# Softmax of the keys with tokens on partitions, their maxima spread by a transfer, in a two-layer linear attention kernel

## The chip, the cores and the metric

The kernel runs on one core of one Trainium2 chip. The metric is the device time of one execution in microseconds (us). A core has TensorE (PE, with its weight loads as PEld), VectorE (DVE), ScalarE (ACT), GpSimd (POOL) and SyncE (SP), which here only issues transfers; each runs its own instructions in the order written, and they wait for each other by semaphores.

## The reference

x has 32 batches of 128 tokens and 512 features. Two layers follow each other; each normalises x, makes queries, keys and values, forms for every head a small matrix from keys and values, applies it to the queries, and ends in a conditioned normalisation and an output product.

```python
xn = layernorm(x)
q = xn @ Wq + bq;  k = xn @ Wk + bk;  v = xn @ Wv + bv
k = where(mask, -inf, k)          # second layer: k + (1 - mask) * -1e6
v = where(mask, 0, v)             # second layer: v * mask
q = softmax(q, axis=-1)           # over the 32 (64) features of a head
k = softmax(k, axis=tokens)       # over the 128 tokens of a batch
attn = einsum('bhse,bhsd->bhed', k, v)
y = einsum('bhtd,bhed->bhte', q, attn)
h = layernorm(y) * (1 + scale) + shift      # scale, shift from the condition
x = x + silu(h) @ Wo + bo
```

The first layer has 16 heads of 32 features, the second 8 of 64. All is float32; the large products are made as three products of a high and a low part (WH, WL for weights, XH, XL for x, HH, HL for h).

## The kernel before

There are 64 steps: batches 0 to 31 of the first layer, then the same of the second, and each engine works through them in a software pipeline. In step s TensorE makes `keys(s)`, `values(s)` and `queries(s)`, `output(s-4)` and `mix(s-2)`; `attention` comes for two batches together in every second step, between queries and output (`attention_at`, TOGETHER). Products are made by `split_product` (line 1152).

Keys are made for a pair of batches at once, turned: a step makes half of the 512 features for both batches of its pair, with features on partitions and 256 tokens in a row, as 24 matmuls of 256 columns. So the softmax over tokens runs along a row. `keys` on VectorE (lines 1575 to 1581) adds the mask, takes the maximum and makes the bias; `exp_k` on ScalarE (829) is four exponentials with their sums; `key_sums` (1587) is the reciprocal, `normalise_keys` on GpSimd (674) the product, `turn_keys` (1596) a turn of 32x32 blocks into KT. Two transfers, out (`write_keys`, `write_half_keys`) and back in four parts (`place_keys`), put tokens on partitions, in EK. `load_mask` and `mask_of_keys` (687, 689) bring the mask to all partitions for each pair. `attention` (1232) writes 16 small products for a batch into the diagonal blocks of a PSUM bank that `zero_attention`, `zero_turned` and `zero_film` keep zero elsewhere, and `heads` on ScalarE (902) copies the bank whole to ATT.

`mix` (1248) multiplies EQ, the exponentials of the turned queries, with ATT. `mixed` on VectorE (1650 to 1664) divides and takes the statistics of y, `root_y` on GpSimd makes the factors, `norm_y` (836) applies them. The queries and y are turned by VectorE into QS (`turn_queries`, `turn_y`), written by `write_qy` and read back into QT by `read_qy`, four transfers behind a wait (434) until `exp_q` (847) and `film` have read the batch before, for QT is one buffer. `film` (867) with its tanh (872) and `h_mul` (1670) make h; `h_high` on ScalarE (916) and `h_low` on GpSimd (680) make HH and HL, for which `output` waits. X is turned in the same manner (`norm_x` 953, `turn_x` 1537, `write_x`, `read_x`, `x_turned` 935 and 942, `x_low` 667), for the pair after. In six steps (2, 3, 9, 13, 17, 21) `conditioning` adds matmuls. Around steps 31 to 36 the weights are changed, and the order there is written out by hand, as at the start and the end.

## Time and profile before

| | us |
|---|---|
| median of 3 runs | 861.52 |
| lowest and highest | 857.33, 862.12 |
| the profiled execution | 857.14 |
| its span, first to last instruction | 855.1 |
| DVE, ACT, POOL busy in the span | 679.3, 603.1, 548.9 |

Busy times are read against the span; the profiled execution has 2.0 us outside its span. It is near the lowest run, 4.4 below the median. The granted TensorE clock was 1.00 throughout, which is 2.4 GHz. A matmul's busy time reaches past the start of the next one, so how long a product takes is read from start to start.

### The profile page before, as it was taken

Reading aid. Unit: us, or ns where it says so; the run is one execution under the profiler, and the core shown is the slowest. Engines: PE = TensorE matmul, PEld = TensorE weight load, DVE = VectorE, ACT = ScalarE, POOL = GpSimd, SP = SyncE. Lnnn points to the kernel's source line nnn. Section 1 sums busy time; section 2 is a strip of 40 time slices with the busy share of each in tenths; the row PEclk is TensorE's granted clock in tenths of the full one; section 3 lists DMA queues with packets and bytes.
Section 4 is the critical chain, followed back from the end, with each engine's and each line's share of the span. In section 5 each row is a group of like instructions: output and inputs, shape, how many; then the busy total and the mean of one; then the engine's idle time right before and its main releaser. Section 6 shows DMA issues by size and latency. Waiting matters only on the chain.

```text
span 855.1 us, 20095 instructions
## 1 busy us (share of the span) xinstructions
PE 838.2 (98%) x6659; PEld 719.9 (84%) x6659; DVE 679.3 (79%) x1362; ACT 603.1 (71%) x1442; POOL 548.9 (64%) x741
## 2 busy tenths in 40 slices
PE   7999999999999999999999999999999999999998
PEld 7778888888888888888878888888888888888886
DVE  6987778778788788778887887787788787787766
ACT  5376687686676776686876886776776686676665
POOL 3467766766766666766767667667667666765641
PEclk9999999999999999999999999999999999999999
DMA  8876676766667756555587556656566656566441
GB/s 309 286 225 201 201 218 199 228 216 205 195 210 208 233 197 199 179 165 175 169 247 233 185 172 200 201 180 201 179 204 201 202 186 189 178 194 211 142 160 62
DMA packets 139404, 169.81 MB, mean 199 GB/s; under 512 B 12302, under 2 KB 112006, under 8 KB 139302
## 3 DMA queue, kind: packets, MB, share of 16 engines
q1 hardware_dynamic: 138512, 167.56, 62.5%
q8 instruction: 53, 0.87, 0.4%
q10 hardware_dynamic: 790, 0.98, 0.4%
q14 instruction: 49, 0.40, 0.2%
HBM read 95.61 MB, written 72.88 MB: 197 GB/s over the span
## 4 chain that ended last, share of the span: by engine, by line
PE 83%; DMA 6%; DVE 4%; issue 2%; SPq 2%; POOL 1%; ACT 1%; DVEq 0%; POOLq 0%; ACTq 0%
PE PS L1152 72%; PE PS L1248 6%; PE PS L1232 3%; DMA X<-in_x 2%; DMA XT<-x_turned 1%; DMA x_turned<-XS 1%; DMA k_turned<-KT 1%; DMA QT<-qy_turned 1%; POOL XL L667 0%; SPq L400 0%; PE PS L1322 0%; DMA EK<-k_turned 0%; DVE BNX L1515 0%; PE PS L1276 0%; PE PS L1291 0%
## 5 line engine op out<-in xcount | busy, mean ns | idle before, releaser
L680 POOL TENSOR_TENSOR HL<-H,HH 128x512 fp32r<-128x512 f32 x60 | 77.5, 1292 | 185.3 <-ACT HH L916 185.3
L867 ACT ACTIVATE Z<-QT,FC,FA 128x128 f32<-128x128 f32 x240 | 99.0, 483 | 87.7 <-DMA QT<-qy_turned 87.7
L1152 PE MATMUL PS<-XH,WH_k 128*128 128x256 f32 x512 | 149.8, 293 | 0.7 <-DVE KN L1581 0.7
L1152 PE MATMUL PS<-XL,WH_k 128*128 128x256 f32 x512 | 144.8, 283 | 0.0
L1152 PE MATMUL PS<-XH,WL_k 128*128 128x256 f32 x512 | 144.8, 283 | 0.0
L953 ACT ACTIVATE XN<-X,NBX,RSX 128x512 f32<-128x512 f32 x60 | 48.8, 813 | 85.5 <-POOL NBX L629 85.5
L829 ACT ACTIVATE SK<-SK,KN 128x128 f32<-128x128 f32 x256 | 98.9, 387 | 10.7 <-DVE KN L1581 10.4
L1152 PE MATMUL PS<-WH_o,HH 128*128 128x512 f32 x248 | 101.3, 408 | 2.0 <-issue 1.9
L1152 PE MATMUL PS<-WH_v,XH 128*128 128x512 f32 x256 | 100.8, 394 | 0.0
L1152 PE MATMUL PS<-WH_q,XH 128*128 128x512 f32 x256 | 100.7, 393 | 0.0
L1152 PE MATMUL PS<-WL_v,XH 128*128 128x512 f32 x256 | 100.3, 392 | 0.0
L1152 PE MATMUL PS<-WL_q,XH 128*128 128x512 f32 x256 | 99.8, 390 | 0.0
L1152 PE MATMUL PS<-WH_v,XL 128*128 128x512 f32 x256 | 99.6, 389 | 0.0
L1152 PE MATMUL PS<-WH_q,XL 128*128 128x512 f32 x256 | 99.6, 389 | 0.0
L1152 PEld LDWEIGHTS PS<-XH,WH_k 128*128 128x128 f32 x512 | 97.9, 191 | 1.3 <-issue 1.1
L1152 PEld LDWEIGHTS PS<-XL,WH_k 128*128 128x128 f32 x512 | 98.2, 192 | 0.1
L1152 PEld LDWEIGHTS PS<-XH,WL_k 128*128 128x128 f32 x512 | 98.1, 192 | 0.0
L1152 PE MATMUL PS<-WL_o,HH 128*128 128x512 f32 x248 | 96.9, 391 | 0.0
L1152 PE MATMUL PS<-WH_o,HL 128*128 128x512 f32 x248 | 96.9, 391 | 0.0
L651 POOL TENSOR_TENSOR X<-X,BB 128x512 f32<-128x512 f32 x64 | 83.8, 1311 | 0.2
L667 POOL TENSOR_TENSOR XL<-XF,XH 128x512 fp32r<-128x512 f32 x60 | 78.1, 1302 | 5.2 <-issue 3.6
L674 POOL TENSOR_TENSOR SK<-SK,RE 128x512 f32<-128x512 f32 x64 | 66.8, 1044 | 19.7 <-DVE RE L1587 19.6
(171 smaller groups left out, 2106.6 us busy)
## 6 DMA issues: line engine op xcount, KB each, us to landing
qy_turned<-QS SPq DMA_DIRECT2D x60, 512.0 KB, 2.9
QT<-qy_turned SPq DMA_DIRECT2D x240, 128.0 KB, 3.1
EK<-k_turned SPq DMA_DIRECT2D x128, 128.0 KB, 2.8
x_turned<-XS SPq DMA_DIRECT2D x30, 512.0 KB, 3.3
XT<-x_turned SPq DMA_DIRECT2D x120, 128.0 KB, 3.5
k_turned<-KT SPq DMA_DIRECT2D x52, 256.0 KB, 3.8
out_x<-X SPq DMA_DIRECT2D x31, 256.0 KB, 3.2
X<-in_x SPq DMA_DIRECT2D x11, 512.0 KB, 5.3
```

The costliest lines, as they stand in the source:

```text
L651: eng.tensor_tensor(X[:, b, :], X[:, b, :], BB[:, 2, :], ALU.add).then_inc(pool_bo, 1)
L667: eng.tensor_tensor(XL[g % 2][:, dst, :], XF0[:, :, :], XH[g % 2][:, dst, :].bitcast(F32), ALU.subtract).then_inc(pool_xl, 1)
L674: eng.tensor_tensor(sk, sk, RE[:, :].unsqueeze(2).to_broadcast([P, 4, T]), ALU.mult).then_inc(pool_kn, 1)
L680: eng.tensor_tensor(hl_of(o), h_of(o), hh_of(o).bitcast(F32), ALU.subtract).then_inc(pool_hl, 1)
L829: e = eng.activation(SK[:, p, a, :], SK[:, p, a, :], ACT.Exp, bias=KN[:, p, t, cc:cc + 1], accum_out=SE[:, p, a:a + 1])
L867: z = eng.activation(z_of(o)[:, c * P:c * P + P].rearrange("p (q n) -> p q n", q=Q), src, ACT.Identity, bias=FC[l][:, c, b:b + 1], scale=F ...
L953: eng.activation(XN[:, t, :], X[:, n % B, :], ACT.Identity, bias=NBX[:, r:r + 1], scale=RSX[:, r:r + 1]).then_inc(act_xn, 1)
L1152: mm = eng.matmul(dst, left[a](c), right[b](c), start=(c == 0 and a + b == 0), stop=(c == C - 1 and a == 1))
L1232: mm = eng.matmul(PS[f:f + 32, bank_att(j), c * P + a:c * P + a + w], vs if l == 0 else ks, ks if l == 0 else vs, start=True, stop=True, t ...
L1248: mm = eng.matmul(bank(B_Y + c // 2, (c % 2) * W, W), EQ[:, c * P:c * P + P], ATT[:, c // 2, (c % 2) * W:(c % 2 + 1) * W], start=True, sto ...
```

## The change

Keys are made like values and queries: tokens on partitions, 12 matmuls of 512 columns for one batch. ScalarE copies them to SK with the mask as a bias for each partition (`keep_keys`, MK). For the softmax over tokens only a common maximum is needed, taken over both batches of a pair separately: `key_maxima` turns 32x32 blocks and reduces them to 16 numbers for each partition, TensorE turns these (`turn_max`), `row_maxima` finishes them in a 32x32 tile, rounded with the bias of the keys as before. The 4 KB are written to HBM (`write_max`) and read back to all partitions (`spread_max`), GpSimd subtracts them (`shift_keys`), and ScalarE takes one exponential (`exp_k`). Nothing is normalised then: values get a column of ones for each head (`slots_of`), so the attention yields the sum beside the products, `scale_heads` on VectorE divides by it, and `heads` on GpSimd writes the block-diagonal ATT by a product with DG, which is zero outside the diagonal (in the second layer the product on VectorE, without the turn; for the last batch VectorE writes the blocks itself). Banks in PSUM needn't be zero, so the memsets go, and so do the masks' transfers and the two key transfers.

Steps now go in pairs of two kinds:

```diff
-            def step(s):
-                keys(s)
-                values(s)
-                (conditioning) queries(s) (fold)
-                for j in attention_at(s):
-                    attention(j)
-                output(s - 4)
-                mix(s - 2)
+            def even_step(s):                 # TensorE
+                keys(s)
+                values(s)
+                keys(s + 1)
+                for j in attention_at(s):     # s - 2, s - 1
+                    attention(j)
+                queries(s)
+                output(s - 4)
+                turn_max(s // 2)
+                mix(s - 2)
+            def odd_step(s):
+                values(s)
+                (conditioning) queries(s) (fold)
+                output(s - 4)
+                mix(s - 2)
```
```diff
+            def even_step(s):                 # VectorE
+                add_x(s - 5)
+                mixed(s - 3)
+                turn_x, turn_queries(s - 1)
+                key_maxima(s)
+                turn_y(s - 3)
+                values(s)
+                scale_heads(s - 2)
+                h_mul(s - 4)
+                stat_x (two)
+                key_maxima(s + 1)
+                queries(s)
+            def odd_step(s):
+                row_maxima(s // 2)
+                h_mul(s - 4)
+                add_x(s - 5)
+                mixed(s - 3)
+                scale_heads(s - 2)
+                turn_queries(s - 1)
+                values(s)
+                turn_x, turn_y(s - 3)
+                queries(s)
```
```diff
+            def even_step(s):                 # GpSimd
+                add_bo(s)
+                root_y(s - 3)
+                add_bo(s + 1)
+                heads(s - 2)
+                h_low(s - 4)
+                x_low(s + 2)
+                queries(s)
+                root_x (two)
+            def odd_step(s):
+                h_low(s - 4)
+                root_y(s - 3)
+                heads(s - 2)
+                x_low(s + 2)
+                shift_keys(s - 1)
+                shift_keys(s)
+                queries(s)
```
```diff
+            def even_step(s):                 # ScalarE
+                norm_x
+                exp_k(s - 2)
+                exp_k(s - 1)
+                keep_keys(s)
+                norm_y(s - 3)
+                film(s - 4)
+                exp_q(s - 2)
+                values(s)
+                h_high(s - 4)
+                keep_keys(s + 1)
+                x_turned(s + 2)
+                film(s - 3)
+            def odd_step(s):
+                h_high(s - 4)
+                exp_q(s - 2)
+                norm_x, x_turned(s + 2)
+                norm_y(s - 3)
+                values(s)
```

SyncE has `write_max` and `spread_max` at the head of an odd step, ahead of `write_x`, `write_qy`, `read_x` and `read_qy`. The new pieces that the prediction speaks of:

```diff
+            def shift_keys(i):                # GpSimd
+                eng.wait_ge(ld_mx, 16 * (i // 2 + 1))
+                eng.tensor_tensor(sk, sk, MX[:, i % 2, :], ALU.subtract)
+            def heads(j):                     # GpSimd
+                eng.wait_ge(dve_hd, j + 1)
+                eng.wait_ge(pe_y, j)
+                for b in range(2):
+                    last = eng.tensor_tensor(dst, src.to_broadcast([P, 2, P // w, w]),
+                                             here.to_broadcast([P, 2, P // w, w]), ALU.mult)
+            def scale_heads(j):               # VectorE, first layer
+                eng.wait_ge(pe_att, j + 1)
+                then(eng.reciprocal(RE[:, :].unsqueeze(2), ps[:, :, w:w + 1]))
+                then(eng.tensor_tensor(kt, ps[:, :, 0:w], re, ALU.mult))
+                eng.wait_ge(pool_att, j)
+                eng.transpose(ht, kt).then_inc(dve_hd, 1)
+            def turn_max(g):                  # TensorE
+                eng.wait_ge(dve_pm, 2 * g + 2)
+                eng.transpose(PS[0:D // 16, B_ATT, 0:P], PM[...], ident[:, :])
```

`attention` takes SK as weights and the widened values as moving data, 33 or 65 columns, in both layers, and waits for `exp_k`. At the start, `mix(0)` now stands behind `values(3)`, not ahead of it, and `row_maxima(0)` follows `x_low(2)` and `x_low(3)` on VectorE.

## Rows read from the trace of the kernel before

**Rows 1.** The page, its first part: busy us, share of the span, instructions.
```profile
PE 838.2 (98%) x6659; PEld 719.9 (84%) x6659; DVE 679.3 (79%) x1362; ACT 603.1 (71%) x1442; POOL 548.9 (64%) x741
```

**Rows 2.** Waits of TensorE, the longest: waiting, releaser, us in total, times, longest.
```profile
PE PS L1305 <- DVE XN L1526: 2.8, 1, 2.8
PE PS L1232 <- DMA EK<-k_turned: 2.2, 2, 1.3
```

**Rows 3.** Timeline of TensorE, first layer: start us, busy us, line, instruction, count.
```profile
246.54 0.36 PE L1152 MATMUL PS<-XH,WH_k 128*128 128x256 f32 x1
...
249.50 0.40 PE L1152 MATMUL PS<-WH_v,XH 128*128 128x512 f32 x1
...
252.24 0.39 PE L1152 MATMUL PS<-WH_q,XH 128*128 128x512 f32 x1
...
255.06 0.78 PE L1232 MATMUL PS<-EK,VV 128*32 128x32 f32 x64
255.77 0.51 PE L1152 MATMUL PS<-WH_o,HH 128*128 128x512 f32 x1
...
271.53 0.36 PE L1152 MATMUL PS<-XH,WH_k 128*128 128x256 f32 x1
```

**Rows 4.** The same in the second layer: mix to mix, two steps apart.
```profile
580.52 1.06 PE L1248 MATMUL PS<-ATT,EQ 128*128 128x132 f32 x8
...
605.69 1.06 PE L1248 MATMUL PS<-ATT,EQ 128*128 128x132 f32 x8
```

**Rows 5.** Groups by form: busy us in total, mean ns of one, idle before and releaser.
```profile
L680 POOL TENSOR_TENSOR HL<-H,HH 128x512 fp32r<-128x512 f32 x60 | 77.5, 1292 | 185.3 <-ACT HH L916 185.3
L658 POOL TENSOR_TENSOR SQ<-SQ,QM 128x512 f32<-128x512 f32 x64 | 67.1, 1048 | 5.5 <-DVE QM L1612 2.1
L1577 DVE TENSOR_REDUCE KM<-SK 128x4 f32<-128x512 f32 x64 | 43.9, 686 | 2.2
L1670 DVE SCALAR_TENSOR_TENSOR H<-H,Z 128x512 f32<-128x512 f32 x62 | 43.0, 693 | 3.3 <-ACT H L872 2.5
L916 ACT ACTIVATE HH<-H 128x512 fp32r<-128x512 f32 x60 | 37.0, 617 | 5.1 <-DVE H L1670 4.0 <-PE PS L1152 1.0
L689 POOL TENSOR_SCALAR MB<-MB 128x256 f32<-128x256 f32 x16 | 17.5, 1095 | 1.3
L1650 DVE RECIPROCAL RQ<-PS 128x16 f32<-128x16 f32 x64 | 16.4, 257 | 15.0 <-PE PS L1248 14.9
```

**Rows 6.** Timeline of ScalarE: the head copy of the first attention above.
```profile
255.59 0.60 ACT L902 ACTIVATE ATT<-PS 128x512 f32<-128x512 f32 x1 [0.41 <-PE PS L1232]
```

**Rows 7.** Timeline of VectorE: two turns, one behind the other.
```profile
261.57 0.68 DVE L1537 STREAM_TRANSPOSE XS<-XN 128x512 f32<-128x512 f32 x1
262.18 0.67 DVE L1547 STREAM_TRANSPOSE QS<-SQ 128x512 f32<-128x512 f32 x1
```

**Rows 8.** Waits of the queue of SyncE, that of the reading of QT.
```profile
SPq L434 <- ACT EQ L847: 71.5, 34, 3.1
```

**Rows 9.** Timeline of the queue of SyncE: reading x back, reading queries and y.
```profile
576.29 2.14 SPq L413 DMA_DIRECT2D XT<-x_turned  x4
...
616.41 1.73 SPq L438 DMA_DIRECT2D QT<-qy_turned  x4
```

**Rows 10.** Timeline of ScalarE: the film that waits for that reading.
```profile
621.39 1.65 ACT L867 ACTIVATE Z<-QT,FC,FA 128x128 f32<-128x128 f32 x4 [1.27 <-DMA QT<-qy_turned]
```

**Rows 11.** Transfers: queue, count, KB of each, median us from issue to landing.
```profile
qy_turned<-QS SPq DMA_DIRECT2D x60, 512.0 KB, 2.9
...
MB<-in_mask SPq DMA_DIRECT2D x30, 128.0 KB, 3.9
...
BB<-in_bias_rows SPq DMA_DIRECT2D x6, 256.0 KB, 8.5
```

**Rows 12.** Timeline of GpSimd at the start: a weight split.
```profile
20.28 1.29 POOL L346 TENSOR_TENSOR WL_q<-X,WH_q 128x512 fp32r<-128x512 f32 x1 [4.33 <-ACT WH_q L819]
```

**Rows 13.** Timeline of VectorE at the same time: a sum of 128x4.
```profile
20.57 1.02 DVE L1579 TENSOR_TENSOR KB<-KM,VC 128x4 f32<-128x4 f32 x1
```

**Rows 14.** Timeline of TensorE: the first mix.
```profile
51.89 1.14 PE L1248 MATMUL PS<-ATT,EQ 128*128 128x132 f32 x8 [0.77 <-issue]
```

More of the change, by code:

```diff
@@ L1123, in _ @@
             values(t2)
+            exp_k(62)
             exp_q(t1)
-            heads(t1)
+            exp_k(63)
             norm_y(t0)
@@ L1408, in _ @@
             keep_busy(B_K, 2)
-            def step(s):
-                keys(s)
+            keys(4)
+            queries(4)
+            values(4)
+            output(0)
+            attention(2)
+            keys(5)
+            mix(2)
+            values(5)
+            turn_max(2)
+            queries(5)
+            attention(3)
+            output(1)
+            mix(3)
+            def even_step(s):
+                keys(s)
+                values(s)
[7 more added lines that the diff above has]
+            def odd_step(s):
                 values(s)
@@ L1417, in step @@
                     conditioning_fold(FILM_SLOTS.index(s))
-                for j in attention_at(s):
-                    attention(j)
                 output(s - 4)
                 mix(s - 2)
-            keys(4)
-            queries(4)
-            values(4)
-            output(0)
-            attention(2)
-            mix(2)
-            for s in range(5, B - 1):
-                step(s)
-            keys(31)
+            for s in range(6, B - 2, 2):
+                even_step(s)
+                odd_step(s + 1)
+            even_step(30)
             values(31)
@@ new lines, in _ @@
+            add_x(26)
+            split_low(eng, 4, [3])
+            mixed(28)
+            scale_heads(29)
+            turn_queries(30)
+            values(31)
+            turn_y(28)
+            queries(31)
+            key_maxima(32)
+            turn_x(35)
+            add_x(27)
+            split_low(eng, 5, [0])
+            mixed(29)
+            split_low(eng, 5, [1])
+            split_low(eng, 5, [2])
+            split_low(eng, 5, [3])
+            turn_queries(31)
+            scale_heads(30)
@@ L1952, in _ @@
-            stat_x(41)
-            key_sums(35)
-            turn_keys(34)
-            turn_keys(35)
-            mixed(33)
-            add_x(31)
-            split_low(eng, 7, [2])
-            turn_queries(35)
-            h_mul(32)
-            split_low(eng, 7, [0])
-            turn_y(33)
-            keys(36)
-            queries(36)
-            turn_x(40)
-            key_sums(36)
-            values(36)
-            turn_keys(36)
-            for s in range(B + 5, NT - 2):
-                step(s)
+            turn_x(37)
```

828 lines of the change are left out of this document (366 added, 462 removed).

## The prediction

> **What bounds the kernel now.** I read the page's busy shares first. TensorE is busy for 838.2 of 855.1 us [rows 1]; because the ends of matmuls are modelled, that share alone proves nothing, so the second view is the list of TensorE's waits. There the longest one in total is 2.8 us, at the start [rows 2]. The third view is TensorE's timeline over one pair of steps of the first layer. The reader should see that the start of each product falls where the one before it stops: keys 2.96 us, values 2.74, queries 2.82, two attentions 0.71, and 24.99 from one even step's keys to the next even step's keys [rows 3]. A pair in the second layer takes 25.17 [rows 4]. So a change can gain only what it takes from TensorE's own work, and loses at once what it makes TensorE wait.
>
> **What TensorE is spared.** Keys are now 12 matmuls of 512 columns, like values, and not 24 of 256. By the rows that is 2.74 in place of 2.96; about 0.06 of the 0.22 is a switch cost that the first product after a mix always pays and that passes to values, so I take 0.16 for each of 64 key products: -10.2 us in all, -0.32 for a pair [rows 3]. The 33rd (65th) column of the values costs nothing visible in an attention of 0.36. Added are 32 turns of the maxima, one matmul of 128 columns each; I take 0.15 (bounds 0.1 and 0.3), +5 us in all. The six memsets in PSUM, the key transposes' two transfers and the masks' transfers go; none of them is in TensorE's list of waits beyond 2.2 us. If nothing else moved, the pair would take 24.8.
>
> **Other engines.** ScalarE loses four exponentials with their sums and the head copy, and gets one copy from PSUM and one exponential, each about the 0.62 of a 512-wide activation [rows 5]. It is relieved. VectorE's total is about unchanged: a turn and a maximum of 0.69 each stay, the small operations become the row maxima (about 0.7 for a pair) and the scaling of heads. GpSimd gets more: the subtraction of the maxima has two full inputs (1.29) where normalising took 1.05, the mask operation (1.1 per pair) goes, and the block-diagonal heads come: two products of 128x256 for each batch. Their lower bound is half of a 512-wide product with a broadcast input, 0.52 each; the upper is the 128x256 mask operation, 1.1 each [rows 5]. A product is the same kind of instruction as the first row, so I take 0.57 each, 1.15 a batch. GpSimd is then busy some 19.5 us of a pair: not the bound, but in many chains.
>
> **The path that decides: attention to output in an even step.** Count from the start of an even step s. keys(s) to 2.8, values to 5.5, keys(s+1) to 8.3, attention of s-2 and s-1 to 9.0, queries to 11.9; then TensorE asks for output(s-4), which needs both halves of H. Now the order of VectorE puts the scaling of the heads of s-2, which waits for the attention of this very step, in front of h_mul(s-4); and GpSimd has heads(s-2) in front of h_low(s-4). The chain: a first attention's result reaches the next engine 0.53 after it starts [rows 3, 6], at 8.8. Scaling is a reciprocal (0.26 or less), a product of 128x128 and a turn of 128x128; between 0.5 (three small ones) and 1.6 (both at 0.69) I take 0.75, to 9.6. h_mul 0.69, to 10.3. HH on ScalarE 0.62 with its handover, to 11.0. HL on GpSimd 1.29 with its handovers, to 12.5 [rows 5]. Queries cover it only to 11.9: a wait of 0.6 in each pair (0.3 to 1.5 by the bounds), where the attention used to follow queries and had no output behind it. With it the pair takes 25.4.
>
> **The loop that may be longer still.** The turned queries and y share one buffer, so the transfer that refills it waits until exp_q has read it; today SyncE already waits 71.5 us for that [rows 8]. Around a pair: film(s-4) and its tanh, then exp_q(s-2), 2.9 us; transfer to film(s-3), one case in the trace being 4.98 [rows 9, 10], of which I take 4.75, as a pair moves about 0.6 MB less; to h_mul(s-3), 2.4; on VectorE h_mul, add_x, the five of mixed, scaling, turn_queries, values, turn_x, which stand in this order in the odd step: 5.7, with back-to-back instructions starting 0.61 apart [rows 7]; then the x transfer out 3.0 [rows 11], the issue of x back, 2.1 [rows 9], which stands in front of the issue for the queries, and 4.75 again to film(s-2). Sum 25.6. It is above 25.4, so I take 25.6 for a pair. It falls to 24.9 if transfers take 4.4, and rises to 26.1 with 4.98.
>
> A rule bears on the same place. A small sum on VectorE with both inputs in SBUF took 1.02 us instead of about 0.2 and ended at 21.59, when the GpSimd instruction that began at 20.28 had ended [rows 12, 13]. The Trainium skill, page "SBUF — State Buffer", section "Who interferes with whom", says the same: a VectorE instruction with two SBUF inputs and a GpSimd instruction that reads SBUF exclude each other for their whole length. By that rule h_mul, which has two SBUF inputs, now meets heads on GpSimd; the trace agrees that one of them must wait. What it costs is the third rival below.
>
> **The sum.** First layer, steps 5 to 30, 13 pairs: nine at +0.6 (25.6 less 24.99), four that carry conditioning matmuls and so are already longer than the loop, at +0.4: +7.0. Second layer, steps 36 to 61, 13 pairs at +0.45 (25.6 less 25.17): +5.9. Start: the first maxima go out after the turn on TensorE at about 37 us; row maxima 1, transfer 2, spread about 4, two subtractions 2.6, three roots of x 3.7, add_bo 1.3, queries 1.05, heads 1.2 with waits before the subtraction gives 57 to 58, while the first mix, which now stands behind values(3), could start at 55; it was at 51.89 with values(3) after it [rows 14]. That is +3, with +1 for the maxima on VectorE ahead of x_low: +4. End: the last maxima must go out and back within the 10.6 us between the turn and the last-but-one attention; the chain is about 11.5: +1. The handover of layers (five steps) is reordered; I put it at 0, between -3 and +4. Sum +18: 857.1 profiled becomes 875. The median of the runs, 861.5, lies 4.4 over the profiled execution; the same distance gives 878 to 880, and I say 878.
>
> **Rivals.**
> (A) Faster: the chain is covered. This needs the chain from attention to HL under 3.5 us after the attention, where I have 4.2, and transfers of 4.4 or less. For it speaks that scaling was priced from neighbours and that 0.6 MB less is moved; against it that h_mul, HH and HL alone are 2.6. Then a pair is 24.8, -0.2 and -0.4: -8, with +4 at the start 853 profiled, 857 as a median; without the loss at the start 853.
> (B) Only the chain counts, the loop is hidden: 25.4 a pair. +0.4 and +0.25 for 26 pairs is +8, with +5 for start and end 870, as a median 874; with a scaling of 0.5 it is about 866.
> (C) GpSimd decides. If heads take 2.2, the chain grows by 0.8 and the pair is 26.2; the same if h_mul loses the shared port to heads and starts up to 1.15 late. +1.2 and +1.0 over 26 pairs is +29, with +5: 891, as a median 895.
> (D) The spread is slow. It copies 4 KB to all partitions, 512 KB in all. The nearest rows are the 128 KB mask copy, 3.9, and the 256 KB bias copies, 8.5 at the crowded start; a 512 KB store takes 2.9 [rows 11]. It decides from the point where it lands after GpSimd is free for it, about 23.5 in the pair; with 4 it lands at 23, with 8.5 at 27.5, and exp_k and the next keep_keys push keys(s+1): about 2 us a pair, 920.
>
> **Chances.** Forecast 0.5, A 0.17, B 0.17, C 0.11, D 0.05. The likeliest gives 878, with 870 to 888 as its own range; eight in ten need B's lower half and C: 860 to 900. A measurement of this kernel can tell about 0.5%, 4.3 us: faster means under 857.2, slower over 865.8. Half of A is faster (0.09); the rest of A and a quarter of B is the same (0.13); slower 0.78.
>
> **What would show it.** In the profile after: key products of 12 matmuls in 2.72 to 2.8; in TensorE's waits a new entry at L1152 or "issue" before output in even steps, some 0.6 to 1 us, 26 times, released by GpSimd's HL; HL's wait named after HH or after the heads; ScalarE's Z still waiting for QT. If TensorE's wait stands before mix instead, heads are the price (C); before keys, the spread or x_low. If the list of waits stays under 10 us, A is right. It would also be wrong if attention with SK as weights took clearly more than 0.36.

## The result and the profile after

The changed kernel takes 920.8 us (median of 4 runs, 916.5 to 921.2) against 859.4 for the kernel before on the same chip: 1.070 times as long, 95% interval 1.065 to 1.076. The forecast was 878, at most 900. The direction was right; the size was missed by 43 us. One of the four runs of m6 below took 1732.4 us and is left out of its median. The profiled execution has a span of 914.7 us against 855.1, so the traces have 59.6 us to account for.

The page of the changed kernel, first part (answers to [rows 1]):
```profile
PE 851.5 (93%) x5923; PEld 687.8 (75%) x5923; DVE 676.9 (74%) x1367; ACT 554.6 (61%) x994; POOL 623.9 (68%) x833
```
Fewer matmuls, yet a longer busy time: 736 of them are gone, but some run at the lower of TensorE's two clocks, as shown below. TensorE is idle for 63 us, not 17. The waits of TensorE, the longest (answers to [rows 2]; waiting, releaser, us in total, times, longest):
```profile
PE PS L1126 <- issue: 24.5, 30, 5.6
PE PS L1221 <- issue: 9.7, 3, 5.9
PE PS L1126 <- DVE VV L1626: 7.4, 2, 5.3
PE PS L1126 <- POOL XL L644: 2.9, 1, 2.9
```
Thirty short waits in one line, and a handful of long ones. The second kind the forecast did not have. Where they lie is read from the starts of five key products on TensorE, keys(2), (6), (30), (38) and (62). Before:
```profile
36.39 0.36 PE L1152 MATMUL PS<-XH,WH_k 128*128 128x256 f32 x1
...
91.35 0.36 PE L1152 MATMUL PS<-XH,WH_k 128*128 128x256 f32 x1
...
398.37 0.36 PE L1152 MATMUL PS<-XH,WH_k 128*128 128x256 f32 x1
...
505.62 0.36 PE L1152 MATMUL PS<-XH,WH_k 128*128 128x256 f32 x1
...
808.36 0.36 PE L1152 MATMUL PS<-XH,WH_k 128*128 128x256 f32 x1
```
After:
```profile
34.91 0.47 PE L1126 MATMUL PS<-WH_k,XH 128*128 128x512 f32 x1
...
117.09 0.78 PE L1126 MATMUL PS<-WH_k,XH 128*128 128x512 f32 x1
...
431.88 0.48 PE L1126 MATMUL PS<-WH_k,XH 128*128 128x512 f32 x1
...
557.86 0.48 PE L1126 MATMUL PS<-WH_k,XH 128*128 128x512 f32 x1
...
864.53 0.48 PE L1126 MATMUL PS<-WH_k,XH 128*128 128x512 f32 x1
```
The differences give the table to which every experiment below is added (us of the profiled execution, one for each kernel; "start" is keys(2) to keys(6), "layer 1" keys(6) to keys(30), "handover" keys(30) to keys(38), "layer 2" keys(38) to keys(62); the median of the runs last). The experiments ran on several chips, on which the kernel before took 857.0 to 859.5.

| kernel | keys(2) | start | layer 1 | handover | layer 2 | rest | span | median |
|---|---|---|---|---|---|---|---|---|
| before | 36.4 | 55.0 | 307.0 | 107.3 | 302.7 | 46.7 | 855.1 | 859.4 |
| after | 34.9 | 82.2 | 314.8 | 126.0 | 306.7 | 50.2 | 914.7 | 920.8 |
| m1 no transfer | 35.1 | 65.6 | 314.2 | 124.7 | 307.1 | 50.8 | 897.4 | 901.6 |
| m2 none in pairs 0 to 2 | 37.2 | 67.6 | 315.5 | 126.3 | 306.7 | 50.2 | 903.4 | 904.6 |
| m3 h first | 34.6 | 81.6 | 312.4 | 129.4 | 301.4 | 50.1 | 909.5 | 910.1 |
| m4 attention first | 35.0 | 82.3 | 310.1 | 126.0 | 304.9 | 50.1 | 908.4 | 910.0 |
| m5 handover swaps | 36.9 | 80.2 | 314.2 | 121.8 | 306.7 | 50.2 | 910.1 | 913.5 |
| m6 busy TensorE | 36.8 | 76.0 | 316.0 | 129.3 | 306.8 | 51.3 | 916.2 | 918.4 |
| m9 start order | 35.3 | 76.9 | 314.7 | 126.6 | 306.8 | 50.2 | 910.5 | 913.3 |
| m11 write before load | 34.8 | 78.9 | 314.4 | 126.6 | 306.7 | 50.1 | 911.5 | 915.0 |
| m10 no maxima | 34.4 | 62.4 | 314.0 | 127.0 | 305.5 | 49.3 | 892.5 | 893.4 |
| m7 four moves | 34.6 | 74.3 | 315.7 | 123.1 | 300.8 | 51.8 | 900.3 | 896.6 |
| m8 no maxima, moves | 33.6 | 55.9 | 310.9 | 110.5 | 299.7 | 50.6 | 861.1 | 863.1 |
| m13 no transfer, moves | 34.5 | 65.8 | 309.1 | 112.5 | 302.4 | 50.7 | 875.0 | 877.3 |
| m12 moves and start | 35.7 | 69.6 | 317.9 | 117.5 | 302.9 | 51.8 | 895.3 | 897.8 |
| m14 handover order too | 35.7 | 65.9 | 321.2 | 123.5 | 305.0 | 51.4 | 902.7 | 901.9 |

Of the 59.6 us, 27.2 are lost at the start (1.5 of it was gained ahead of keys(2)), 18.7 in the handover, 3.4 at the end, and only 7.8 and 3.9 in the two steady stretches, on which nearly the whole forecast was built. The table has its own noise: keys(2) itself begins anywhere from 33.6 to 37.2, and m5, which changes nothing before the handover, shows a start of 80.2 for 82.2 although its keys(6) begins at 117.2, as after the change (117.1). So small differences at the start are read below from when keys(6) begins.

**The steady pair.** Timeline of TensorE in the changed kernel, a pair of the first layer (answers to [rows 3]):
```profile
224.06 0.48 PE L1126 MATMUL PS<-WH_k,XH 128*128 128x512 f32 x1
...
229.59 0.39 PE L1126 MATMUL PS<-WH_k,XH 128*128 128x512 f32 x1
...
232.41 0.79 PE L1196 MATMUL PS<-VV,SK 128*32 128x33 f32 x64
...
236.76 0.47 PE L1126 MATMUL PS<-WH_o,HH 128*128 128x512 f32 x1 [0.63 <-issue]
...
249.59 0.48 PE L1126 MATMUL PS<-WH_k,XH 128*128 128x512 f32 x1
```
The pair takes 25.53 us against 24.99 [rows 3], and output(s-4) waits 0.63 in it. The 24.99 was not a typical pair: of the eight pairs before without conditioning between keys(6) and keys(30), five took 24.85 to 24.89. The releaser is named "issue", that is, by nothing on TensorE's own list; what ended last is found on the other engines at that time (here HL, at 236.66):
```profile
232.94 0.18 DVE L1579 RECIPROCAL RE<-PS 128x4 f32<-128x4 f32 x1 [2.46 <-PE PS L1196]
...
233.72 0.65 DVE L1664 SCALAR_TENSOR_TENSOR H<-H,Z 128x512 f32<-128x512 f32 x1
233.88 1.54 POOL L665 TENSOR_TENSOR ATT<-HT,DG 128x256 f32<-128x256 f32 x2 [4.91 <-DVE HT L1596]
234.40 0.63 ACT L896 ACTIVATE HH<-H 128x512 fp32r<-128x512 f32 x1 [1.43 <-DVE H L1664]
235.38 1.28 POOL L673 TENSOR_TENSOR HL<-H,HH 128x512 fp32r<-128x512 f32 x1
```
From the attention at 232.41: scaling begins 0.53 later, h_mul 0.78 after that, HH 0.68, HL 0.98 (HH had ended at 235.03, but the heads ran on GpSimd until 235.42), output 1.38: 4.35 in all. In the second layer a pair takes 25.57 with a wait of 0.3, before 25.17 [rows 4].

**The start.** SyncE's queue, GpSimd, ScalarE, VectorE and TensorE around the first transfer of the maxima, in order of time:
```profile
37.25 0.50 SPq L454 DMA_DIRECT2D k_maxima<-NM  x1
...
43.60 0.34 SPq L461 DMA_DIRECT2D MX<-k_maxima  x1
...
48.10 2.49 POOL L651 TENSOR_TENSOR SK<-SK,MX 128x512 f32<-128x512 f32 x2 [9.81 <-DMA MX<-k_maxima]
...
49.40 0.63 ACT L818 ACTIVATE SK<-SK 128x512 f32<-128x512 f32 x1 [8.37 <-POOL SK L651]
...
53.09 0.67 ACT L812 ACTIVATE SK<-PS,MK 128x512 f32<-128x512 f32 x1
...
53.79 0.71 DVE L1555 STREAM_TRANSPOSE KT<-SK 128x512 f32<-128x512 f32 x1 [7.96 <-ACT SK L812]
...
55.16 0.67 DVE L1626 TENSOR_TENSOR VV<-PS,BB 128x512 f32<-128x512 f32 x1
...
55.89 0.79 PE L1126 MATMUL PS<-WH_v,XH 128*128 128x512 f32 x1 [5.35 <-DVE VV L1626]
```
This is how one exposed transfer walks through in-order queues. The maxima are written at 37.25; the spread can be issued only when the write has landed, at 43.60, and lands itself at 48.1. GpSimd has stood still for 9.8 us; on ScalarE exp_k(0) waits for it and keep_keys(3) stands behind; on VectorE key_maxima(3) waits for that and values(2) stands behind; and TensorE's values(3), which needs nothing of the maxima, waits 5.35 us for its bank. The first mix begins at 61.0, before at 51.9 [rows 14]. The second round trip does it again:
```profile
76.84 0.34 SPq L461 DMA_DIRECT2D MX<-k_maxima  x1
...
81.91 2.48 POOL L651 TENSOR_TENSOR SK<-SK,MX 128x512 f32<-128x512 f32 x2 [5.84 <-DMA MX<-k_maxima]
...
85.66 1.27 POOL L673 TENSOR_TENSOR HL<-H,HH 128x512 fp32r<-128x512 f32 x1
...
87.03 0.77 PE L1126 MATMUL PS<-WH_o,HH 128*128 128x512 f32 x1 [5.59 <-issue]
87.59 0.63 PE L1126 MATMUL PS<-WL_o,HH 128*128 128x512 f32 x1
88.02 0.63 PE L1126 MATMUL PS<-WH_o,HL 128*128 128x512 f32 x1
```
Here h_low(0) stands behind shift_keys(2) and (3) on GpSimd, and output(0) waits 5.59 us. The reader should also see the last two rows: 0.43 us from one matmul to the next. In the steady pair it is 0.23:
```profile
583.74 0.40 PE L1126 MATMUL PS<-WL_k,XH 128*128 128x512 f32 x1
583.97 0.39 PE L1126 MATMUL PS<-WH_k,XL 128*128 128x512 f32 x1
```
After these waits TensorE goes on at its lower level, 1.2 instead of 2.4 GHz (the granted clock is 0.52 from 55.89 to 61.04 and 0.55 from 87.03 to 92.06), and a product of 12 takes 4.4 to 5.2 us instead of 2.7.

One more wait stands in this stretch, that of attention(3), 2.52 us until 104.47. The profile names values on ScalarE, but those are values(5), which it does not need. The code has attention(3) wait for row_maxima(2) (line 1191), since turn_max(2) writes the bank that it needs, and row_maxima(2) ended on VectorE at 104.32. The experiments below bear this out.

**The handover.** GpSimd, SyncE's queue and TensorE of the changed kernel, in order of time:
```profile
453.13 1.73 POOL L356 TENSOR_TENSOR WL_k<-STAGE,WH_k 128x512 fp32r<-128x512 f32 x1
...
454.89 1.28 SPq L365 DMA_DIRECT2D STAGE<-in_wv  x3
...
466.99 0.76 PE L1126 MATMUL PS<-WH_v,XH 128*128 128x512 f32 x1 [0.96 <-DVE WL_v L356]
...
472.92 0.50 PE L1126 MATMUL PS<-WH_v,XH 128*128 128x512 f32 x1 [2.02 <-DVE VV L1626]
...
478.07 0.22 POOL L590 TENSOR_SCALAR VEX<-MVX 128x1 f32<-128x1 f32 x1 [7.26 <-DVE MVX L1496]
...
479.40 1.27 POOL L673 TENSOR_TENSOR HL<-H,HH 128x512 fp32r<-128x512 f32 x1
...
480.76 0.77 PE L1126 MATMUL PS<-WH_o,HH 128*128 128x512 f32 x1 [3.24 <-issue]
```
The three chunks of the value weight are loaded when GpSimd has split the second chunk of the key weight, and values(32) begins before its later chunks are split; values(33) waits for the bank, output(28) for HL(28). HL(28) itself is late because it stands on GpSimd behind root_x(37), which waits 7.26 us for statistics that VectorE takes only behind two splits of the query weight.

### The profile page after: what moved, and what is told of

It reads as the page before. It is cut to its first block, busy times and chain, and to the rows that moved or that the text cites. A ratio compares the mean times of both kernels' runs of the same rounds, so it can differ in the third digit from the quotient of the medians.

```text
span 914.7 us, 18202 instructions
## 1 busy us (share of the span) xinstructions
PE 851.5 (93%) x5923; PEld 687.8 (75%) x5923; DVE 676.9 (74%) x1367; ACT 554.6 (61%) x994; POOL 623.9 (68%) x833
## 4 chain that ended last, share of the span: by engine, by line
PE 77%; issue 7%; POOL 5%; DVE 5%; ACT 3%; DMA 2%; SPq 1%; ACTq 0%; POOLq 0%; DVEq 0%
PE PS L1126 67%; PE PS L1221 5%; PE PS L1196 3%; DMA X<-in_wq 1%; POOL SK L651 1%; POOL XL L644 1%; DMA k_maxima<-NM 1%; POOL HL L673 1%; ACT Z L854 1%; POOL RSY L593 0%; DMA MX<-k_maxima 0%; POOL WL_o L356 0%; POOL SQ L635 0%; DVE WL_v L356 0%; PE PS L1297 0%
## 5 line engine op out<-in xcount | busy, mean ns | idle before, releaser
L665 POOL TENSOR_TENSOR ATT<-HT,DG 128x256 f32<-128x256 f32 x124 | 84.4, 701 | 117.5 <-DVE HT L1596 60.4
L1126 PE MATMUL PS<-WH_v,XH 128*128 128x512 f32 x256 | 105.1, 410 | 8.3 <-DVE VV L1626 7.4
L1126 PE MATMUL PS<-WH_k,XH 128*128 128x512 f32 x256 | 103.9, 406 | 4.3 <-POOL XL L644 2.9
L1126 PE MATMUL PS<-WL_k,XH 128*128 128x512 f32 x256 | 100.8, 394 | 0.0
L1126 PE MATMUL PS<-WH_k,XL 128*128 128x512 f32 x256 | 100.6, 393 | 0.0
L651 POOL TENSOR_TENSOR SK<-SK,MX 128x512 f32<-128x512 f32 x64 | 80.9, 1286 | 16.6 <-DMA MX<-k_maxima 16.6
L635 POOL TENSOR_TENSOR SQ<-SQ,QM 128x512 f32<-128x512 f32 x64 | 67.9, 1061 | 31.2 <-DVE QM L1614 31.0
L818 ACT ACTIVATE SK<-SK 128x512 f32<-128x512 f32 x64 | 40.3, 632 | 79.5 <-POOL SK L651 79.4
L823 ACT ACTIVATE YN<-YN,NBY,RSY 128x512 f32<-128x512 f32 x61 | 49.8, 816 | 63.7 <-POOL NBY L616 63.7
L1126 PEld LDWEIGHTS PS<-WH_o,HH 128*128 128x128 f32 x248 | 47.9, 193 | 45.5 <-issue 36.5
```

The costliest lines, as they stand in the source:

```text
L635: eng.tensor_tensor(sq, sq, QM[:, 0:D // w].unsqueeze(2).to_broadcast([P, D // w, w]), ALU.subtract)\
L651: eng.tensor_tensor(sk, sk, MX[:, i % 2, :], ALU.subtract).then_inc(pool_kn, 1)
L665: last = eng.tensor_tensor(dst, src.to_broadcast([P, 2, P // w, w]), here.to_broadcast([P, 2, P // w, w]), ALU.mult)
L818: eng.activation(sk, sk, ACT.Exp).then_inc(act_ek, 1)
L823: eng.activation(y, y, ACT.Identity, bias=NBY[:, :], scale=RSY[:, :]).then_inc(act_yn, 1)
L1126: mm = eng.matmul(dst, left[a](c), right[b](c), start=(c == 0 and a + b == 0), stop=(c == C - 1 and a == 1))
```

## The experiments

**Is it the transfer?** Edits of m1 and m2 (SKIP is all pairs in m1, range(3) in m2):
```
 def write_max(g), def spread_max(g):      + if g in SKIP: return
 def shift_keys(i):                        + if i // 2 in SKIP: return
 def exp_k(i):  - wait pool_kn   + wait act_ka and dve_pm (skipped pairs)
```


> The changed kernel without write_max, spread_max and shift_keys for all 32 pairs: the maxima are still formed (two turns, reductions, turn_max, row_maxima), but the exponential is taken of the unshifted keys, so the subtraction of the maximum is what is left out. Theory R (round trips): the 25.7 us that the first six samples lost come from the three waits for MX at the start (9.8, 5.8 and 0.9 us in shift_keys) and what queues behind them; then the start gives back some 18 to 24 us, the handover between the layers keeps its 18.7, a pair keeps 25.5, and the time is 895 to 903. Theory S (the order of the start): the start is slow because of the order in which its steps stand, whoever waits; then it gives back under 8 us and the time stays above 912. Theory P (GpSimd's load): 2.6 us of work less in a pair on GpSimd shortens every pair too; then keys to keys of a pair falls below 25.2 and the time goes to 890 or less.

> As the kernel without the transfer, but only pairs 0 to 2 (keys 0 to 5) are left unshifted; from pair 3 on everything is as in the changed kernel. Theory R: the same 18 to 24 us come back as at the start without any transfer, keys(6) begins near 95 instead of 117 us, and everything after it is as it was: 897 to 903. Theory S: keys(6) begins at 110 or later, 912 or more.


Measured: 901.6 and 904.6 us (1.051 and 1.054 times before). The start falls from 82.2 to 65.6 and 67.6, and keys(6) begins at 100.7 and 104.8 instead of 117.1: the round trips cost 12 to 17 us, nearly all of it in the first three pairs. That is theory R, smaller than it said (18 to 24, with keys(6) near 95); m2 stays outside its 897 to 903. Behind keys(6) little changes: handover 124.7, a pair 25.5, and also the rest at the end (50.8 against 50.2), so the last transfer does not cost the 3.4 us there. GpSimd is spared 2.6 us a pair, and a pair does not move: theory P falls. Of the start's 27.2 us, 10.6 stay.

**What sets the steady pair?** m3, and m4, which undoes one half of the change:
```
 m3, DVE even_step            m3, GpSimd even_step     m4, TensorE even_step
-  scale_heads(s - 2)        -  heads(s - 2)           values(s)
   h_mul(s - 4)                 h_low(s - 4)          -keys(s + 1)
+  scale_heads(s - 2)        +  heads(s - 2)           attention(s - 2), (s - 1)
                                                      +keys(s + 1)
```


> In even steps h_mul(s-4) goes before scale_heads(s-2) on DVE and h_low(s-4) before heads(s-2) on GpSimd, nothing else moves. Theory C (my prediction's chain from the attention over the scaling to h_mul, the head copy and h_low to output(s-4)): output(s-4) no longer waits for the scaling, its wait of 0.5 to 0.8 us in each even step goes, a pair falls from 25.55 to 24.8 to 25.0, and 27 steady pairs give back 15 to 20 us: 901 to 906. Theory L (the loop over film, exp_q, read of the turned queries and y): the wait moves to another place of the pair and a pair stays at 25.4 to 25.6: 917 to 922.

> In even steps both attentions go ahead of the second keys on TensorE, nothing else moves (this undoes the second half of the change). Moving h_mul and h_low ahead of the scaling had given pairs of 24.65 us in the first layer and 25.0 in the second, against 25.53 and 25.57. Theory C (the chain attention, scaling, h_mul, head copy, h_low, output): the attention begins 2.8 us earlier against output(s-4), the slack covers the 0.65 and 0.38 us of the wait, and pairs are the same 24.65 and 25.0: 903 to 909. Theory O (the exponentials of s-2 and s-1 come too late for an attention that stands 2.8 us earlier): PE waits for SK in front of the attention instead, 0.3 us or more a pair, and a pair stays above 25.3: 913 or more.


Timeline of TensorE in m3, the pair that was shown above for the changed kernel:
```profile
221.69 0.48 PE L1126 MATMUL PS<-WH_k,XH 128*128 128x512 f32 x1
...
230.03 0.79 PE L1196 MATMUL PS<-VV,SK 128*32 128x33 f32 x64
...
233.60 0.39 PE L1126 MATMUL PS<-WH_o,HH 128*128 128x512 f32 x1
...
246.34 0.48 PE L1126 MATMUL PS<-WH_k,XH 128*128 128x512 f32 x1
```
The wait is gone and the pair takes 24.65 us; in the second layer it takes 24.98 to 25.0. m4, by the other way, the earlier attention, gives 24.63 to 24.73 and 24.97 to 25.02 in the pairs that nothing else delays. Two different ways of sparing the chain from the attention through the scaling give the same pair, so that chain set it: theory C. The loop of my forecast is refuted for the steady pair, since nothing holds it at 25.4 or more. In TensorE's list of waits the first line changes thus:
```profile
PE PS L1126 <- issue: 16.7, 10, 3.8
```
Twenty waits are gone. Both kernels take 910, though, not 901 to 906 and 903 to 909, as some pairs got longer, in m3 those whose steps carry conditioning (30.5 and 28.6 us in place of 27.3 and 27.5) and the handover (129.4). In the first of these the film at 255.22 waits 2.55 us for QT, and output(s-4) at 260.64 waits 2.22: the wait for QT is the loop's, so it seems to bind after a disturbance, not in the steady pair; no run separates this. m4 keeps 4.7 us in layer 1 but only 1.8 in layer 2, where four pairs took 25.7 to 26.8; why those did was not tried.

**The handover, two swaps.**
```
 GpSimd: - root_x(37)  h_low(28)            + h_low(28)  root_x(37)
 DVE:    - split 6 [0],[2]  stat_x(37),(38) + stat_x(37),(38)  split 6 [0],[2]
```


> Two swaps at the handover between the layers, nothing else: on GpSimd h_low(28) before root_x(37), on DVE stat_x(37) and stat_x(38) before the splits of weight 6. Theory W (the splits of the weights stand in front of what output(28) needs): output(28) begins at some 474 instead of 480.8 us, and keys(34) 4 to 7 us earlier: 914 to 917. Theory D (whoever stands behind the splits of weight 5 in values(32) and (33) sets the stretch, so that what output(28) gains is lost to the next wait): under 2 us, 919 to 921.


Measured: 913.5 us. keys(32) to keys(34) falls from 49.84 to 44.57, and output(28) begins at 476.5 instead of 480.8; theory W, with less than it said for output(28). The root and the statistics of a batch that nothing needs soon had stood ahead of h_low(28), for which TensorE waited.

**The clock.** m6 changes no order; its extra matmuls, read by nobody, stand where TensorE waited:
```
 attention(0)   + 18 matmuls      values(3)
 values(4)      + 20 matmuls      output(0)
 queries(5)     + 9, + 18         around attention(3), output(1)
 handover:      + 5 to 10 before values(32), (33), output(28), queries(33),
                  output(29), mix(31) and behind it
```


> The changed kernel with small extra matmuls (128x128, of the identity, into banks that are free, read by nobody) in the places where TensorE waited: three at the start (after attention(0), before output(0), around output(1)) and along the handover between the layers; no order changes. Theory K (a good part of the lost time is TensorE's own clock: after each wait the products go at 1.2 GHz, 12 matmuls in 4.4 to 5.1 us instead of 2.7, seven of them in the handover and four or five at the start): the granted clock stays near 1 there and 8 to 16 us come back: 899 to 907. Theory N (the slow products only fill time in which the other engines are late anyway): the wait gets longer as the products get shorter, and the time stays within 4 us of the changed kernel, 911 to 921.


Measured: 918.4 us, theory N by the time. Busy time of each engine from 50 to 120 and from 450 to 510 us, with the granted clock behind the parenthesis of POOL, the changed kernel first:
```profile
50.00:120.00 70.00, 48.75 (x329) 37.96 (x330) 36.98 (x77) 31.13 (x55) 41.28 (x55) 0.83 0.35 110
450.00:510.00 60.00, 45.42 (x236) 34.61 (x235) 37.83 (x78) 28.73 (x51) 35.21 (x44) 0.89 0.55 171
```
```profile
50.00:120.00 70.00, 62.35 (x481) 52.66 (x481) 39.04 (x80) 33.84 (x60) 45.07 (x58) 0.95 0.35 113
450.00:510.00 60.00, 53.31 (x372) 44.88 (x374) 37.12 (x77) 27.70 (x49) 34.67 (x44) 0.97 0.50 158
```
In the handover the clock rose from 0.89 to 0.97, values(33) took 2.85 us and not 4.6, and the stretch got no shorter (129.3 against 126.0): the slow products lay in waits for other engines. The extra matmuls stand in TensorE's own queue and may have cost a part of what the clock gave; that was not separated. At the start keys(6) begins 4.3 us earlier (112.8), of which the time kept 2. A mean clock of 0.979 looks like 19 us lost; by this run at most a few of them come back.

**The order at the start.**
```
 m9  GpSimd: root_x(7), (8), (9), add_bo(0) ahead of shift_keys(0), (1)
     ACT:    exp_q(0), norm_x(6), (7), values(1), split 3 ahead of exp_k(0)
     DVE:    values(2) ahead of key_maxima(3)
 m11 SP:   - load_w(3)  write_max(0)  spread_max(0)
           + write_max(0)  spread_max(0)  load_w(3)
```


> Only the start: on GpSimd root_x(7) to root_x(9) and add_bo(0) go before shift_keys(0), on ACT exp_q(0), norm_x(6), norm_x(7), values(1) and the split of weight 3 before exp_k(0), on DVE values(2) before key_maxima(3). Theory Q (the 9.8 us wait for the first transfer costs most by what is queued behind it): values(3) begins 3 to 5 us earlier, and keys(6) 4 to 8 us: 907 to 912. Theory T (the transfer itself stands on the path, through exp_k(0), attention(0) and the slot of keys(3)): keys(6) moves by under 2 us, 913 to 921.

> Only the order on SP at the start: write_max(0) and spread_max(0) ahead of the load of weight 3 (1 MB), which the changed kernel issues 0.4 us before the write. Theory B (the first transfer waits in the DMA engines behind the megabyte): the write lands 3 us or more earlier, shift_keys(0) begins at 42 to 45 instead of 48.1 us, and keys(6) 2 to 5 us earlier, unless the weight's split then comes late. Theory R (write, landing, issue and spread each cost their own latency, about 11 us in all whatever stands ahead): shift_keys(0) begins at 46.5 or later and the time stays within 2 us of the changed kernel.


Measured: 913.3 and 915.0 us. In m9 values(3) begins at 51.8 and not 55.9, and keys(6) 4.9 us earlier: theory Q by these, though the time lies 1.3 above its range; what is queued behind the transfer is a part of its price. In m11 the spread is issued at 40.8 instead of 43.6 and the first subtraction begins at 45.3 instead of 48.1, keys(6) 3.4 us earlier. That is theory B, just short of the 3 us and the 42 to 45 that it gave. The time from the write's issue to the spread's falls from 6.35 to 4.07 us, against 1.35 in most later pairs, so the megabyte was one part of it; what the rest is was not tried (a load of 2 MB had been issued at 30.0).

**Without any maxima.** m10 leaves out key_maxima, turn_max, row_maxima, write_max, spread_max, shift_keys and exp_k:
```
-eng.activation(SK[:, i % 3, :], PS[:, bank_k(i), :], ACT.Identity, bias=MK[:, l, b:b + 1]).then_inc(act_ka, 1)
+eng.activation(SK[:, i % 3, :], PS[:, bank_k(i), :], ACT.Exp, bias=MK[:, l, b:b + 1]).then_inc(act_ka, 1)
```

> The changed kernel with no maxima of the keys at all: key_maxima, turn_max, row_maxima, write_max, spread_max and shift_keys go, and the bias step takes the exponential itself (so the subtraction of the maximum is left out, and one pass on ACT goes with it). Orders otherwise as in the changed kernel. Theory C (the scaling chain alone sets the steady pair): a pair still shows the wait before output(s-4) and takes 25.0 to 25.5 us; with the start as without the transfer (keys(6) near 95) and a handover of 16 to 18 us over before: 884 to 898. Theory M (the maxima's load on DVE, GpSimd and ACT makes the chain late): the wait before output(s-4) goes too, pairs of 24.6 and 25.0 us, 870 to 884. If both the start and the handover stay as long as without the transfer, neither of them is the maxima's, but comes from the order of the changed kernel.


Measured: 893.4 us. A pair takes 25.44, with 0.56 of wait before output: theory C; the maxima's load has at most 0.1 us of a part in it. The start falls only to 62.4, the handover stays at 127.0. So in this order of the kernel neither the handover's 18.7 nor the last 7.4 us of the start need the maxima.

**The moves together, with and without the maxima.** m7 and m8, beside the edits of m3, m5 and (in m7) m9:
```
 (c) DVE odd_step(5):    scale_heads(3) ahead of turn_x, turn_y, queries(5)
     GpSimd odd_step(5): heads(3) ahead of root_x(10), shift_keys(4), queries(5)
     TensorE:            attention(3) ahead of queries(5)
 (d) ACT:    x_turned(34) ahead of film(29), exp_q(31), norm_y(30) ahead of x_turned(35)
     GpSimd: x_low(34) ahead of heads(31), root_y(30) ahead of queries(32)
```


> The changed kernel, nothing left out, with four moves whose effects lie in stretches of their own: (a) h_mul and h_low ahead of the scaling in even steps, as tried alone; (b) the order of the start as tried alone; (c) scaling and heads of sample 3 ahead of turn_x, turn_y, queries(5), root_x(10) and shift_keys(4), and attention(3) ahead of queries(5); (d) the handover: the two swaps tried alone, and besides x_turned(34) ahead of film(29) and exp_q(31) ahead of norm_y(30) on ACT, x_low(34) ahead of heads(31) and root_y(30) ahead of queries(32) on GpSimd. Theory O (the handover is long because of the order on ACT and GpSimd, and the start's last 8 us because mix(3) stands behind heads(3)): keys(32) to keys(34) falls from 44.6 (swaps alone) to 38 or less, keys(5) to keys(6) from 24.3 to 16 to 19, pairs 24.65 and 25.0: 886 to 895. Theory D (both stretches are bound by transfers: weights, turned x, maxima): keys(32) to (34) stays at 43 or more and keys(5) to (6) at 22 or more: 898 to 905.

> As the kernel without any maxima (their formation, their transfer and their subtraction are left out), with the moves (a), (c) and (d) of the kernel beside it, but not the order of the start (b). Theory O: 893 less 15 (pairs of 24.65 and 25.0 for 25.44), less 5 (keys(5) to keys(6)), less 10 or more (handover): 858 to 868, so that keys with tokens on partitions do at best what the kernel before does, even with the maxima free. Theory D: the start and the handover stay, 875 to 880.

> The kernel with the four moves, and the transfer of the maxima and shift_keys left out for all pairs as in the first experiment (the maxima are formed but not subtracted). The same four moves with no maxima at all gave 863 us, with everything 897. This splits the 34 us. Theory X (the exposed transfers at the start and what stands behind them are most of it): keys(2) to keys(6) falls from 74.3 to 58 or less, the handover (keys(30) to (38), 123.1) by under 4 us, time 876 to 882. Theory F (forming the maxima, two turns and two reductions a pair on DVE and an exponential of its own on ACT, costs in the handover and the film pairs): the handover stays above 119, and what is left to 863 lies there and in keys(6) to keys(30). Theory G (it is the transfer, the shift on GpSimd above all, that stretches the handover too): keys(30) to (38) falls to 112 to 115 and the time to 865 to 872.


m13 is m7 with the skips of m1. Measured: 896.6, 863.1 and 877.3 us; before 858.9. Without maxima, moves (a), (c) and (d) take the start from 62.4 to 55.9 (keys(5) to keys(6) from 20.3 to 14.0) and the handover from 127.0 to 110.5: theory O, order it was. With the maxima the same moves leave 74.3 and 123.1; m7 lies between its two theories, with 42.5 for keys(32) to keys(34) and 20.9 for keys(5) to keys(6). m13 lies between: start 65.8, as in m1, and handover 112.5. Its time is what theory X gives, but the start is not at X's 58 or less, and the handover falls by 10.7 us, as theory G has it; of these, 5.8 are in keys(36) to keys(38), which took 31.1 us in m7 and 25.4 in m13. In the unrepaired kernel, leaving out the transfer had moved the handover by 1.3 only. The two causes hide each other: as long as the order holds the stretch, the transfer costs nothing there, and once it is mended, the transfer shows.

Why the start does not profit in m13 is in its trace: attention(3), which (c) puts ahead of queries(5), begins at 90.80 after a wait of 5.25 us, and row_maxima(2) had ended at 90.65. In m7 the two are 100.03 and 99.88, in m1 91.31 and 91.17. m8 and m10 have no maxima, hence no turn in that bank and no such wait, and there attention(3) does not wait; in m8 it begins at 82.12, 4.6 us ahead of values(5) on ScalarE. So move (c) paid only where the maxima were gone.

**The last two.** m12 is m7 with m11's edit, 12, 20 and 8 extra matmuls in the start's waits, and attention(3) behind queries(5) again; m14 gives TensorE in the handover the order of the kernel before (output(28), turn_max(16), mix(30), queries(32) between values(32) and values(33); output(29) behind keys(34)); VectorE and ScalarE follow it.
```
 m12, TensorE, start              m14, TensorE, handover
  attention(0)                     values(32)
 +keep_busy(B_Q, 12)              -values(33)
  values(3)                        output(28)  turn_max(16)  mix(30)  queries(32)
  ...                             +values(33)
  values(4)                        queries(33)
 +keep_busy(B_O, 20)              -output(29)
  output(0)                        mix(31)  keys(34)
  ...                             +output(29)
  queries(5)                       values(34)  keys(35)
 +keep_busy(B_K, 8)
  attention(3)
```


> The kernel with the four moves, nothing left out, and three more at the start: the first write and spread ahead of the load of weight 3, small extra matmuls (read by nobody) in TensorE's two long waits at the start, and queries(5) back ahead of attention(3). Alone, the first gave keys(2) to keys(6) 3.3 us and the second 6.2 us. Theory A (they add up on the path through the start): keys(6) begins at 98 to 102 instead of 108.9 us, 888 to 892. Theory B (the second round trip, formed at 71, landed at 77 to 79, sets keys(6) whatever is gained before it): under 3 us, 894 to 899.

> The best kernel with the maxima so far (nothing left out; extra matmuls at the start are read by nobody), and on TensorE the order of the handover as in the kernel before: between values(32) and values(33) stand output(28), turn_max(16), mix(30) and queries(32), and output(29) comes behind keys(34); DVE and ACT follow it (values(33) behind queries(32) on DVE, behind h_high(29) on ACT). Theory O (the long handover comes from two products of the new layer back to back, each with a wait for its weights or for the bank, and from the old layer's outputs queued behind them): keys(30) to keys(38), 117.5 and 123.1 us in the two kernels with the old order and 107.3 before the change, falls to 109 to 114, and the time by 4 to 10 us: 888 to 894. Theory W (the weights' splits and loads set it, whatever TensorE's order): 116 or more, and the time within 3 us of 897.


Measured: 897.8 and 901.9 us. In m12 the start is 4.8 us shorter (keys(5) to keys(6) falls from 20.9 to 16.1 with attention(3) back behind queries(5)), and the time is not: layer 1 got 2.2 longer, and m7's profiled execution, 902.1, lies 5.5 above its own median, so that the two traces can't be set against each other to a few us. By its time it is theory B. m14 does not help: values(32) waits 0.95 us for its weights, output(28) 5.04 for HL(28), keys(34) 4.12 for XL, and the handover takes 123.5. So TensorE's own order is not the cause by itself. The last of these waits is for x_low(35) on GpSimd, which in my arrangement stands behind queries(33). It is theory W by the stretch (116 or more), though the time is 4 to 5 above and not within 3 of 897; that the splits and loads set the stretch, as W says, is not shown. How the handover of the kernel with its maxima could come back to 107 is open.

## Why the prediction was wrong

**Right, within 0.2 us:** a key product takes 2.82 (2.96 less the 0.16 I took gives 2.80); the turn of the maxima 0.11, inside its bounds; scaling to h_mul 0.78, taken at 0.75; attention to output 4.35, taken at 4.2; the wait 0.63, taken at 0.6; heads on GpSimd 1.19, or 1.54 when they meet h_mul, taken at 1.15. A first-layer pair took 25.53, a second-layer pair 25.57, for 25.6. Layer 1 lost 7.8 in 12 pairs (forecast 7.0 in 13) and layer 2 3.9 in 12 (5.9 in 13). The four pairs with conditioning lost 0.3 to 0.9 each, taken at 0.4.

**Right number, wrong reason:** I took 25.6 from the loop over film, exp_q and the transfers, against 25.4 from the chain. m3 and m4 took the chain away and left 24.65 and 25.0. The loop is at least 0.95 shorter than its sum; which of its terms was too long was not measured. That the pair came out at 25.53 for a forecast of 25.6 is luck. It was rival B that happened in the pair, 0.1 to 0.2 over its 25.4. Rivals C and D did not, and that D's 920 is the measured time is chance: heads took 1.2 to 1.5 and not 2.2, with 2.6 us less on GpSimd a pair stays at 25.5 (m1), and the spread lands in 3.6 us, in a pair's slack:
```profile
MX<-k_maxima SPq DMA_DIRECT2D x32, 512.0 KB, 3.6
```

**Mis-sized, the start:** +4 in the sum, +25.7 at keys(6), by size the largest miss. Three things went wrong. The write was priced at 2 and took 6.35 until the spread could be issued, in part because of a megabyte of weights ahead of it; so the first mix begins at 61.0, where the forecast had 57 to 58. Then I stopped at the first mix. The second round trip, 71 to 82, adds 6 until keys(5), as HL(0) is queued behind it; and another 11.7 come until keys(6), where odd_step(5) puts heads(3) behind turns, queries and root_x(10) (moving them gives back 6.4 without the maxima, m10 to m8) and where attention(3) waits for the maxima. Along one path through the runs, the 27.2 us are 16.6 of round trips (m1), 3.2 of forming the maxima (m1 to m10), 6.5 of order (m10 to m8) and 0.9 of rest. Another path gives another split: with the maxima formed but not sent, the moves give nothing (65.6 in m1, 65.8 in m13), and then leaving out the forming gives 9.9 (m13 to m8).

**Not worked out, the handover:** "reordered; I put it at 0, between -3 and +4". It is +18.7. No number stood behind it: TensorE's order alone was read, and not which split, root or film stands ahead of what on the three other engines. Shown is that order on GpSimd, VectorE and ScalarE costs 16.5 us without the maxima (m10 to m8) and 12.2 with them formed but not sent (m1 to m13), that two swaps give back 4 with everything in place (m5), that a higher clock alone did not shorten it (m6), and that with the order mended the transfer costs 5 to 11 there (m7 and m12 to m13). Not shown is an order that would bring the stretch back with the maxima in it.

**Mis-sized, the end:** +1 for the last transfer, +3.4 measured, and 4.1 without a transfer (m1), 2.6 without any maxima (m10). What it is was not tried.

**Could the change gain?** In the steady pairs, a little: with the wait gone they take 24.65 and 25.0, against 24.85 to 24.99 and 25.17. But layer 1 as a whole never came below its 307.0 of before (309.1 in m13 is the least), as the pairs with conditioning got longer; layer 2, 302.7 before, took 299.7 (m8) to 305.0 (m14). The best kernel with its maxima takes 896.6 (1.045 times before, 1.041 to 1.050), and even with the maxima free the time is 863.1 (1.007, 1.003 to 1.011). No version here beats the kernel before.

**The shared port:** heads beside h_mul, as at 233.88 above, take 1.54 us or more for the two, in 28 of 62 cases; in m3, where h_mul has passed before, they take 1.18 to 1.20 in 60 of 62. The Trainium skill, page "SBUF — State Buffer", section "Who interferes with whom", which the forecast named, makes the shared port pair an exclusive lock. The trace agrees: h_mul had begun 0.16 us earlier and kept its 0.65, and GpSimd, 0.49 us of which lie beside it, paid 0.35. C's price of up to 1.15 on h_mul did not occur, but VectorE paid elsewhere: the last subtraction of row_maxima(2), a 32x32 one with two inputs in SBUF, took 1.15 us from 103.17, against 0.18 mostly, while x_low ran on GpSimd from 102.96 to 104.28, and attention(3) waited for it.

## What to carry to other kernels

Steady stretches are forecast well from rows of the trace; a start and a handover are not steady stretches at a discount, and must be walked through instruction by instruction on every in-order queue, above all where a transfer's round trip is new: its price is its latency in each queue that has something unrelated behind the wait. Write a number for every reordered stretch, or widen the range by what its waits can reach; "between -3 and +4" for five steps, without a row behind it, was one of the two large errors. And when a wait is removed, look for the cause that it had hidden: causes in one stretch don't add up.

## What was unexpected of the hardware

A clock below 1 was here more a symptom than a cause. TensorE's granted clock was 0.83 from 50 to 120 us, with matmuls 0.43 us apart instead of 0.23 after waits of 5 us; raising it from 0.89 to 0.97 in the handover by extra matmuls did not shorten it. A transfer of 4 KB written and read again is mostly cheap in a steady pair (1.35 us from the write's issue to that of the spread, at 371.90 and 373.25; 3.50 at the most, from 600.06) and took 6.35 us at the start behind a load of 1 MB, 4.07 with the load issued after it (m11, 36.75 to 40.82).
